# Cross attention: folds in pairs between the halves of the Wo and context products

## The reference

```python
# x: (64, 64, 256), context: (64, 256, 256), 16 heads of 64
q = (query @ Wq + bq).reshape(b, sq, 16, 64)        # query = layernorm(x)
k = (key @ Wk + bk).reshape(b, 256, 16, 64)         # key = value = context
v = (value @ Wv + bv).reshape(b, 256, 16, 64)
scores = einsum('bqhd,bkhd->bhqk', q, k) / 8
attn = softmax(scores)
out = einsum('bhqk,bkhd->bqhd', attn, v).reshape(b, sq, 1024) @ Wo + bo + query
x = x + layernorm(out) * gamma + beta
```

## Time and profile before

| | |
|---|---|
| median of the runs | 2296.89 us |
| the profiled execution | 2297.97 us, its span 2296.2 us |
| TensorE (PE) busy | 2151.3 us (94%) |
| VectorE (DVE) busy | 1584.7 us (69%) |
| ScalarE (ACT) busy | 1267.9 us (55%) |
| GpSimd (POOL) busy | 709.7 us (31%) |
| one group of four batches, between its equal points | 88.44 us |

### The profile page before, as it was taken

The page is one execution under the profiler, slowest core; times in us unless marked ns, Lnnn a source line. Parts: engine busy times, 40 slices in busy tenths (PEclk is TensorE's granted clock), DMA queues, the critical chain, the costliest instruction groups (busy, mean ns, idle before and its releaser), DMA issues. The chain is left out here.

```text
span 2296.2 us, 48591 instructions
## 1 busy us (share of the span) xinstructions
PE 2151.3 (94%) x16836; PEld 1870.7 (81%) x16837; DVE 1584.7 (69%) x2992; ACT 1267.9 (55%) x3071; POOL 709.7 (31%) x677
## 2 busy tenths in 40 slices
PE   6999999999999999999999999788897996999997
PEld 6888888888888888888888888667775885888886
DVE  6767767767768667677677676578885755666665
ACT  5656555555556556555565555356664334555554
POOL 4001001001011010010010010367774274777775
PEclk9999999999999999999999999899997998999999
DMA  4001001000010010010010001252224221333332
GB/s 145 15 15 33 14 18 32 6 26 23 9 32 23 9 32 18 14 32 18 14 32 14 18 10 40 85 182 76 78 76 163 82 86 39 54 53 54 55 53 44
DMA packets 103215, 104.41 MB, mean 45 GB/s; under 512 B 14064, under 2 KB 92656, under 8 KB 103152
## 3 DMA queue, kind: packets, MB, share of 16 engines
q1 hardware_dynamic: 87280, 84.62, 11.7%
q0 software_dynamic: 15872, 18.95, 5.2%
HBM read 72.73 MB, written 30.81 MB: 45 GB/s over the span
## 5 line engine op out<-in xcount | busy, mean ns | idle before, releaser
L534 ACT ACTIVATE probs<-banks,nbias 128x256 f32<-128x256 f32 x512 | 235.6, 474 | 231.7 <-DVE nbias L664 231.3
L876 PE MATMUL banks<-ctxT_hi,qk_hi 128*128 128x256 f32 x1024 | 302.0, 295 | 0.0
L876 PE MATMUL banks<-ctxT_hi,qk_lo 128*128 128x256 f32 x1024 | 290.4, 284 | 0.0
L876 PE MATMUL banks<-ctxT_lo,qk_hi 128*128 128x256 f32 x1024 | 289.3, 282 | 0.0
L622 DVE TENSOR_TENSOR pT_lo<-banks,pT_hi 128x512 fp32r<-128x512 f32 x256 | 166.4, 685 | 165.2 <-ACT pT_hi L496 163.8
L496 ACT ACTIVATE qk_hi<-banks 128x512 fp32r<-128x512 f32 x256 | 139.7, 619 | 153.7 <-PE banks L919 150.7
L622 DVE TENSOR_TENSOR qk_lo<-banks,qk_hi 128x512 fp32r<-128x512 f32 x256 | 158.8, 682 | 86.7 <-ACT qk_hi L496 86.7
L876 PE MATMUL banks<-pT_hi,ctx_hi 128*128 128x512 f32 x512 | 208.0, 406 | 3.9 <-DVE pT_lo L622 2.9
L422 POOL TENSOR_TENSOR rstd<-mv,power 128x2 f32<-128x2 f32 x32 | 22.2, 693 | 603.1 <-DVE mv L705 603.1
L876 PE MATMUL banks<-pT_hi,ctx_lo 128*128 128x512 f32 x512 | 202.1, 395 | 0.0
L876 PE MATMUL banks<-pT_lo,ctx_hi 128*128 128x512 f32 x512 | 200.9, 392 | 0.0
(11 more groups left out here) (258 smaller groups left out, 5955.8 us busy)
## 6 DMA issues: line engine op xcount, KB each, us to landing
ctx_raw<-in_ctx_dram SPq DMA_DIRECT2D x64, 256.0 KB, 2.7
experts_w<-in_L_ffn_We_dram SPq DMA_DIRECT2D x24, 512.0 KB, 8.3
x_in<-in_x_dram SPq DMA_DIRECT2D x16, 256.0 KB, 2.9
x_again<-in_x_dram SPq DMA_DIRECT2D x16, 256.0 KB, 2.8
x_stream<-z SPq DMA_DIRECT2D x16, 256.0 KB, 2.2
s_x<-x_stream SPq DMA_DIRECT2D x32, 128.0 KB, 2.1
s_x_again<-x_stream SPq DMA_DIRECT2D x32, 128.0 KB, 2.1
x_normalised<-s_xl SPq DMA_DIRECT2D x32, 128.0 KB, 1.7
```

Of the source, the lines that this page charges most:

```text
L534: nc.scalar.activation(probs[:, s % 2, p, :], scores[:, s % 2, p // 2, (p % 2) * SK:(p % 2 + 1) * SK], ACT.Exp, bias=nbias[:, s % 2, p:p + ...
L876: last = nc.tensor.matmul(out, a, b, start=(n == 0), stop=(n == 3 * len(pairs) - 1))
```

## The change

`EARLY` goes. In steps 3 and 7 the folds are taken two at a time, and between the pairs stand the halves of the other products. The function `part_of_pc` says which half of the context product stands ahead of fold pair i: in step 3 half c = i - 2, in step 7 half c = i - 1.

- Ring and TensorE, step 3: o 0, folds 0 1, o 1, folds 2 3, pc 0, folds 4 5, pc 1, folds 6 7.
- Ring and TensorE, step 7: folds 0 1, pc 0, folds 2 3, pc 1, folds 4 5, qbk, folds 6 7.
- ScalarE takes the same order. Its exponentials stand at the head of step 3; in step 7 they stand behind folds 0 and 1, as before.
- VectorE takes the same order; in step 7 folds 0 and 1 stand ahead of the peaks, behind the context's lower half.

```diff
+def part_of_pc(half, i):
+    c = i - (1 if half else 2)
+    return c if 0 <= c < DC else None
...
 # ring_order
-        if s == 3 and g.prev:
-            out += [("o", t) for t in range(TILES)]
-        if b == 3 and (g.next if half else g.cur):
-            out += [("fold", half, h) for h in range(EARLY)]
-        if (g.cur if s >= 2 else g.prev):
+        if b == 3:
+            for i in range(HALF // 2):
+                c = part_of_pc(half, i)
+                if s == 3 and g.prev and i < TILES:
+                    out.append(("o", i))
+                if g.cur and c is not None:
+                    out.append(("pc", s, c))
+                if s == 7 and g.next and i == 3:
+                    out.append(("qbk",))
+                if (g.next if half else g.cur):
+                    out += [("fold", half, h) for h in (2 * i, 2 * i + 1)]
+        elif (g.cur if s >= 2 else g.prev):
             out += [("pc", s, c) for c in range(DC)]
-        if b == 3 and (g.next if half else g.cur):
-            out += [("fold", half, h) for h in range(EARLY, HALF)]
-        if s == 7 and g.next:
-            out.append(("qbk",))
...
 # ScalarE
-                if b == 3 and (g.next if half else g.cur):
-                    for h in range(EARLY):
-                        fold_upper(g, half, h)
-                if g.cur:
+                if g.cur and s < STEPS - 1:
                     exps(g, s)
...
+                if b == 3:
+                    for i in range(HALF // 2):
+                        c = part_of_pc(half, i)
+                        if g.cur and c is not None:
+                            copy_pc(g, s, c)
+                        if (g.next if half else g.cur):
+                            for h in (2 * i, 2 * i + 1):
+                                fold_upper(g, half, h)
+                        if g.cur and s == STEPS - 1 and i == 0:
+                            exps(g, s)
...
 # VectorE
                 if s == STEPS - 1 and g.next:
                     ctx_lower(g, b)
+                    for h in range(2):
+                        fold_lower(g, half, h)
                 if g.cur:
                     peaks(g, s)
...
+                if b == 3:
+                    for i in range(half, HALF // 2):
+                        if s == 3 and g.prev and i < TILES:
+                            bank, free = wait_filled(dve, g, ("o", i))
+                            nc.vector.tensor_tensor(z[:, i, :], bank[:, 0:D], resid[:, i, :], ALU.add).then_inc(free, 1)
+                        if s == 7 and g.next and i == 3:
+                            keep_qbk(g)
+                        if (g.next if half else g.cur):
+                            for h in (2 * i, 2 * i + 1):
+                                fold_lower(g, half, h)
...
 # TensorE: do_pc takes the halves to compute, do_o one half; then as in ring_order
+                if b == 3:
+                    for i in range(HALF // 2):
+                        c = part_of_pc(half, i)
+                        if s == 3 and g.prev and i < TILES:
+                            do_o(g, i)
+                        if g.cur and c is not None:
+                            do_pc(g, s, [c])
+                        if s == 7 and g.next and i == 3:
+                            do_qbk(g)
+                        if (g.next if half else g.cur):
+                            do_fold(g, half, (2 * i, 2 * i + 1))
```

More of the change, by code:

```diff
@@ L41 @@
 RING = 4
-EARLY = 2
 LINKS_PER_GROUP = 39
@@ L536, in exps, with copy_pc @@
                                      accum_out=rsum[:, s % 2, p:p + 1]).then_inc(exp_done, 1)
-        def copy_out(g, key, out, rows):
-            bank, free = wait_filled(act, g, key)
-            nc.scalar.activation(out, rows(bank), ACT.Identity).then_inc(free, 1)
+        def copy_pc(g, s, c):
+            at = slice((s + 2) % GB * SQ, ((s + 2) % GB + 1) * SQ)
+            bank, free = wait_filled(act, g, ("pc", s, c))
+            nc.scalar.activation(pc[:, c, :, at], bank.rearrange("p (h q) -> p h q", h=HALF),
+                                 ACT.Identity).then_inc(free, 1)
         for g in turns(act):
@@ L589, in scalar @@
                         q_upper(g, half, m)
-                if (g.cur if s >= 2 else g.prev):
-                    at = slice((s + 2) % GB * SQ, ((s + 2) % GB + 1) * SQ)
+                if b == 3:
[8 more added lines that the diff above has]
+                            exps(g, s)
+                elif (g.cur if s >= 2 else g.prev):
                     for c in range(DC):
[L593 to L596, removed]
+                        copy_pc(g, s, c)
                 if (g.cur if s >= 1 else g.prev):
@@ L922, in do_fold, with do_pc @@
                 last.then_inc(done, 1)
-        def do_pc(g, s):
+        def do_pc(g, s, parts=range(DC)):
             b = (s + 2) % GB
@@ L934, in do_pc @@
                 pe.wait_ge(ctx_split, GB * g.at + b + 1)
-            for c in range(DC):
+            for c in parts:
                 bank, done = bank_for(pe, g, ("pc", s, c))
@@ L964, in do_v, with do_o @@
                 last.then_inc(done, 1)
-        def do_o(g):
+        def do_o(g, n):
             for j in range(2):
                 wait_freed(pe, g, ("v", 0, j))
[L969 to L974, removed]
+            bank, done = bank_for(pe, g, ("o", n))
+            for m in range(HALF):
+                last = nc.tensor.matmul(bank[:, 0:D], oT[:, m, n * P:(n + 1) * P], wo[:, m, :],
+                                        start=(m == 0), stop=(m == HALF - 1))
+            last.then_inc(done, 1)
         def do_xT(g):
```

## The result

The changed kernel took 2348.11 us (median of five runs, 2346.13 to 2348.59); the kernel before, run beside it, 2295.93 us. The ratio is 1.0228, with a 95% interval of 1.0214 to 1.0242. The profiled execution took 2346.13 us, its span 2344.4 us, which is 48.2 us more than the span of before. The forecast was 2342 us, its range 2304 to 2360.

A forecast was written before the change was run, and what follows sets the result against it. TensorE's dense stream, busy 94% of the span, was taken as the bound, held up in step 7. 17.1 - 6.4 + 2.5 + 37.5 - 4.8 = +45.9 us on the median 2296.9 gave 2342 us, range 2304 to 2360.

The forecast's parts named there:

- The stall of step 7: Cross attention, step 7: TensorE idles 2.47 us before fold 4; 1.14 us lost in each of 15 groups, +17.1 us.
- the forecast's signs: Expected in the new profile: in step 7, transposes about 12 us after fold 0's start instead of 10.9.
- Step 3: Cross attention, step 3 in 15 groups with Wo products: waits for ring banks go, -0.43 us each, -6.4 us.
- my bound of -8 us: Largest gain allowed for step 3 in 15 groups, if switches between products cost nothing.
- the old holes: TensorE's waits in step 3 before the change, counted as 0.55 us in all with switches of bank.
- Group 0: Step 3 of the first group, with no Wo product to cover the exponentials: +2.5 us, once.
- The clock: Falls of TensorE's granted clock behind nearly every step 7: +37.5 us, less 4.8 for three earlier falls.
- three cases: Cost of a clock fall by where it comes: early 2.3 us, middle 3.3, late 1.7; mean rounded up to 2.5.
- second case: Outcome by the skill's clock rule: clock falls no more often than before, +13 us, 2310 us; chance 0.19.
- Stalls without the clock: Rival: step 7 stalls, but the clock falls no more often than before; +13 us, 2310 us; chance 0.19.
- The interleaving pays in step 7 too: Rival: step 7's exponentials begin by 638.5 and its holes close; -46 us, 2251 us, half effect 2274; chance 0.08.
- stalls-only case: Lower end of the forecast range, given as 2304 us; the rival without more clock falls was summed to 2310.

The follow-up runs named there:

- the gap filled: The changed kernel with ten unread 512-column products on TensorE between the second context half and fold 4 of step 7; ratio 1.0049 to the kernel before.
- the kernel with step 3 alone: The changed kernel with step 7 put back to its order of before on every engine, only step 3 interleaved; ratio 0.9996 to the kernel before.
- the peaks first: The changed kernel with VectorE again taking the peaks of step 7 ahead of fold subtractions 0 and 1; ratio 0.9999 to the kernel before.
- step 7 alone: The changed kernel with step 3 put back to its order of before, only step 7 changed; ratio 1.0266 to the kernel before.
- that kernel: The changed kernel with step 7's peaks behind four folds and exponentials behind six, group 0's step 3 exponentials behind folds 0 and 1; ratio 0.9898 to the kernel before.

## Why the prediction was right

**The stall of step 7** was worked out as +1.14 us a group, from a fold 4 that starts 7.83 us after fold 0. It started 7.82 us after, with exponentials at 5.35 as worked out. The price by difference is 1.2 us a group, and 1.15 by the stretch from fold 0 to the transposes. Those transposes came 14.07 us after fold 0 and not the 12 us of the forecast's signs, because the low clock already lies over the qbk products; with the gap filled they came after 12.03. The cause is confirmed from two sides: move the copy of context half 0 ahead of the exponentials, or bring the exponentials 1.2 us earlier, and ScalarE no longer stops TensorE there. What I hadn't worked out is that undoing VectorE's order alone puts a wait of 1.4 us in another place, with a fall of the clock behind it.

**Step 3** gave 0.60 us a group with itself alone (0.65 by its stretch in the changed kernel), where I had 0.43. Both are more than my bound of -8 us for the 15 groups allowed: I charged 0.1 us for a second change between the Wo products and the folds, which cost nothing, and counted the old holes 0.1 short. **Group 0** cost 3.4 us by its qbk products in the kernel with step 3 alone, not 2.5. TensorE's gap there was 3.08 us, and a low clock from 67.3 to 70.7 us starts 0.2 us behind its end, which I had not put there.

**The clock** was the largest term and the least certain, +37.5 us less 4.8. By difference, up to the last qbk products, it is about 41 us for 14 groups: they take 91.95 us on average, and 89.05 with the gap filled. The filled gap shows the low clock to be a cause and not a companion: the stall stays and the time goes. The size was near because most falls were of 6.8 us, as assumed; the mean of three cases had been drawn a little low, 2.5 us for the 2.9 measured on average and 3.05 in the groups of equal length. That the falls would be of this length rested on one stretch of before, and that there would be one at every step 7 on three falls behind smaller holes; neither was worked out, and there luck had a part.

**The rule of the Trainium skill** that was weighed ("TensorE: Matmul & The Clock Gate", Part 1) would have kept the clock up behind a gap of this size; that is the forecast's "second case", the stalls without the clock. The runs say otherwise: a gap of 2.4 us with thin work behind it was followed by a fall in 15 of 15 cases, and one wait of 1.4 us in 13 of 15.

**The rivals.** "Stalls without the clock" would have been 2310 us; the kernel with the filled gap is that case, at a ratio of 1.0049, 11 us over before, where the 13 us of the rival are 1.0057. "The interleaving pays in step 7 too" had the right deciding point, the time at which context copy 0 is done: where it is done ahead of the exponentials, the kernel is 0.9% to 1.4% faster. The changed kernel misses it by 2.4 us.

The sum fell 6 us short of the median (2342 for 2348.11) and 2.3 us short of the change in span: +45.9 for +48.2. The terms erred both ways: the clock and group 0 were put too low, step 3's gain too. One slip is in the range: its lower end, 2304, is called the stalls-only case, which the same text adds up to 2310.

## What to carry to other kernels

When several engines share a small ring of buffers, ask of every reordering which buffer is held over a long wait of its reader, and which instruction needs that buffer next; here the cure was to let ScalarE take four to six folds, and the context halves between them, while it waited for its exponentials anyway. What is gained in one step can come back in the next, as it did in four kernels here, so look at the distances of all steps. A stall on TensorE can have a second price, the clock behind it, which no list of waits shows: compare the granted clock and the distance between equal points of successive groups. A single sub-step can be judged from that distance to 0.1 us where the total is too noisy.

## What was not expected of the hardware

- With a fall of the clock in nearly every group the groups were nearly equal all the same: 92.03 to 92.11 us in ten of 15 intervals of the changed kernel, 88.74 to 88.77 us in 12 of 15 with the peaks first. The kernel before is as even without falls (88.42 to 88.45 us in 11 of 15), and with step 7 alone the intervals go round from 92.4 to 93.4 us, so it isn't shown that the clock sets the distance.
- The qbk products at a granted clock of 0.50 took twice their time, 2.6 us (849.62 to 852.21) for 1.36 before, although they have only 16 columns each.
- A VectorE instruction of 4 columns took 1.20 us beside a GpSimd instruction on SBUF (0.16 alone). In that kernel all 16 of these that start under GpSimd's split of the context take 0.88 to 1.22 us and end 0.02 us behind it, as the two rows above show; the other 112 take 0.16. VectorE's 512-column subtraction out of PSUM beside the same kind of GpSimd work took its usual 0.68 us. That GpSimd holds VectorE up is argued from these times; it wasn't tested by itself.
